# Spreading the loads of x and of the mixing weights over the expert slots, and a loading depth of three groups in the last stage of a two-layer mixture kernel

## What is computed

```python
x = x + L0_ffn(L0_cond(x, cond_128, ...), W_gate, b_gate, W_e, b_e)      # mean of relu(x @ W_e + b_e) over the top 2
x = x + L1_ffn(L1_cond(x, cond_128, ...), qweight, scales, zeros, bias)  # (mix_b @ x_b) @ (scales * q - zeros) + bias
```

## Time and profile before

| | us |
|---|---|
| median of 3 timed runs | 529.42 (529.12 to 530.06) |
| the profiled execution's own time | 527.31 |
| its span, first to last instruction | 525.5 |
| TensorE busy | 499.7 (95% of the span) |
| VectorE busy | 347.2 (66%) |
| ScalarE busy | 121.3 (23%) |
| GpSimd busy | 152.8 (29%) |

### The profile page before, as it was taken

One profiled execution on the slowest core, in us unless ns is written; L12 is line 12 of the kernel. 1 busy time (PEld: TensorE's weight loads), 2 busy tenths in 40 slices (PEclk: granted clock), 3 DMA queues, 4 the chain that ended last, 5 costly groups with the idle time before them and its releaser, 6 DMA issues. The chain is left out here.

```text
span 525.5 us, 10384 instructions
## 1 busy us (share of the span) xinstructions
PE 499.7 (95%) x2412; PEld 332.3 (63%) x2413; DVE 347.2 (66%) x1082; ACT 121.3 (23%) x277; POOL 152.8 (29%) x178
## 2 busy tenths in 40 slices
PE   6999999999999987999999999999997599999996
PEld 5999999999954433444444444444445477777774
DVE  3688888888865637574443545443346499999996
ACT  3233333334411101111111111111123112222220
POOL 9144444444446222232333232332223000000000
PEclk9999999999998998999999999999998989999999
DMA  4979978999766795556666656565435988988522
GB/s 118 286 206 306 299 255 274 345 362 319 211 179 204 221 269 140 137 145 176 181 174 172 166 162 178 173 188 146 141 111 202 334 312 277 291 286 276 204 83 100
DMA packets 91440, 113.06 MB, mean 215 GB/s; under 512 B 25438, under 2 KB 62222, under 8 KB 90372
## 3 DMA queue, kind: packets, MB, share of 16 engines
q1 hardware_dynamic: 73200, 71.26, 47.9%
q0 software_dynamic: 11664, 36.24, 18.9%
q10 hardware_dynamic: 6536, 5.10, 3.6%
HBM read 67.55 MB, written 46.52 MB: 217 GB/s over the span
## 5 line engine op out<-in xcount | busy, mean ns | idle before, releaser
L1190 PE MATMUL bank<-we,lT 128*128 x536 | 235.4, 600 | 4.5 <-DVE ring_a L929 4.5
L1190 PEld LDWEIGHTS bank<-we,lT 128*128 128x128 f32 x536 | 102.4, 192 | 132.8 <-issue 132.6
L540 POOL DMA_INDIRECT pairs_d<-ring_b,pair_i x71 | 70.7, 995 | 166.2 <-DVE pair_i L918 97.9
L929 DVE TENSOR_TENSOR ring_a<-bank,be_bc 128x512 f32<-128x512 f32 x71 | 49.0, 691 | 104.0 <-PE bank L1190 59.2
L1163 PE MATMUL bank<-wconv,phases 128*128 128x128 f32 x768 | 91.4, 276 | 0.7 <-ACT phases L566 0.7
L619 ACT ACTIVATE ring_b<-ring_a 128x512 f32<-128x512 f32 x71 | 44.8, 631 | 201.2 <-DVE ring_a L929 185.8
L1163 PEld LDWEIGHTS bank<-wconv,phases 128*128 128x128 f32 x768 | 88.7, 192 | 0.9 <-ACT phases L566 0.9
L523 POOL DMA_INDIRECT lists_d<-token_list,row_i x64 | 62.9, 982 | 83.3 <-DVE row_i L839 48.4
L915 DVE STREAM_TRANSPOSE lT<-xt 128x512 f32<-128x512 f32 x71 | 49.9, 703 | 10.5 <-DMA keys<-lists_d 8.9
L1257 PE MATMUL bank<-wq,high 128*128 128x512 f32 x128 | 38.9, 427 | 3.4 <-PEq L1205 3.4
L1151 PE MATMUL bank<-wg,lT 128*128 128x136 f32 x256 | 37.4, 289 | 1.1 <-DVE partial L810 1.1
(11 more groups left out here) (194 smaller groups left out, 401.7 us busy)
## 6 DMA issues: line engine op xcount, KB each, us to landing
xt<-lists_d SPq DMA_DIRECT2D x284, 64.0 KB
xt<-in_x SPq DMA_DIRECT2D x60, 256.0 KB
we<-pairs_d SPq DMA_DIRECT2D x28, 512.0 KB, 5.0
we<-in_L_ffn_W_e SPq DMA_DIRECT2D x8, 1024.0 KB
out<-orow_list SPq DMA_DIRECT2D x32, 256.0 KB, 3.7
lists_d<-orow_list SPq DMA_DIRECT2D x8, 257.0 KB
be_bc<-in_L_ffn_b_e ACTq DMA_DIRECT2D x4, 512.0 KB
words<-pairs_d POOLq DMA_DIRECT2D x4, 512.0 KB, 5.4
```

The source lines that it names most:

```text
L540: pool.indirect_dma_start(pairs_d, bass.IndirectOffsetOnAxis(ap=pair_i[:, s % DR:s % DR + 1], axis=0), ring_b[:, s % U, :], None, bounds_c ...
L929: dve.tensor_tensor(ring_a[:, j % 2, :], ps_exp[j % 2][:, :], be_bc[:, bass.ds(expert, 1), :].rearrange("p a n -> p (a n)"), ALU.add).then ...
L1190: mm = pe.matmul(ps_exp[j % 2][:, :], lT[:, j, p * P:(p + 1) * P], we[:, bass.ds(expert, 1), p, :].rearrange("m a n -> m (a n)"), start=(p ...
```

## The change

Four edits.

- SyncE, stage 2: the loads of x of groups 0 to 3 no longer stand together after `list_step(7)`; one stands after each of `list_step(16)` to `list_step(19)`. The unrolled part of SyncE's loop is longer by 12 slots for this.
- ScalarE, stage 2: the two loads of the mixed biases move from slot 8 to slot 9; the four loads into `mix_bd` move from slot 8 to slots 11, 15, 19 and 23, one in each. ScalarE's unrolled part is longer by 16 slots.
- SyncE, start of stage 3: x of group 4, then pairs 4, x 5, pairs 5, x 6, pairs 6, in place of four loads of x and eight of pairs. The waits for the scatters stay with pairs 4, 5 and 6.
- SyncE, `row_step(g)`: after the store of group g it loads x and pairs of group g + 7 (DEPTH = 3), in place of x of g + 8 and pairs of g + 12.

No transfer is added or taken away; the sizes and the buffers are the same. The programs of VectorE, TensorE and GpSimd are unchanged.

```diff
--- before.py
+++ after.py
@@ -31,6 +31,7 @@
 U = 4
 XR = 4
 FR = 8
+DEPTH = 3
 DR = 8
 LK = L + 2
 NO_PAIR = 1 << 20
@@ -435,11 +436,12 @@
                                      ).then_inc(list_in[ja], 16)
                     sp.dma_start(keys[:, ja, :], lists_d[bass.ds(row, P), L:LK]).then_inc(list_in[ja], 16)
 
-            for s in range(-U, lo2):
+            for s in range(-U, 20):
                 list_step(s, s % U)
-            for g in range(PRIMED):
-                sp.dma_start(htok[:, g, :], x_g[g]).then_inc(x3_in[g % XR], 16)
-            stepped(sp, list_step, lo2, lo2, hi2 - U, NT - U)
+                if s >= 16:
+                    g = s - 16
+                    sp.dma_start(htok[:, g, :], x_g[g]).then_inc(x3_in[g % XR], 16)
+            stepped(sp, list_step, 20, 20, hi2 - U, NT - U)
 
             def load_x(a):
                 sp.dma_start(xt[:, a % XR, :], x_g[a]).then_inc(x3_in[a % XR], 16)
@@ -448,25 +450,24 @@
                 sp.dma_start(found[:, a % FR, :, :], pairs_g[a]).then_inc(pairs_in[a % FR], 16)
 
             sp.wait_ge(lT_ready, NT)
-            for g in range(PRIMED, PRIMED + XR):
-                load_x(g)
+            load_x(PRIMED)
             sp.wait_ge(exp_done, NT)
-            for g in range(PRIMED, PRIMED + FR):
-                if filled_by(g - 1) < NT:
-                    for i, done in enumerate(result_out):
-                        sp.wait_ge(done, 16 * len(range(i, min(filled_by(g), NT), U)))
+            for g in range(PRIMED, PRIMED + DEPTH):
+                for i, done in enumerate(result_out):
+                    sp.wait_ge(done, 16 * len(range(i, min(filled_by(g), NT), U)))
                 load_pairs(g)
+                if g + 1 < PRIMED + DEPTH:
+                    load_x(g + 1)
 
             def row_step(g, j):
                 sp.wait_ge(out_ready, g + 1)
                 sp.dma_start(out_g[g], orow[:, j % 2, :]).then_inc(out_out[j % 2], 16)
-                a, b = g + PRIMED + XR, g + PRIMED + FR
-                if live(a, NG):
-                    sp.wait_ge(ya_ready, a - XR + 1)
+                a = g + PRIMED + DEPTH
+                if a < NG:
+                    wait(sp, ya_ready, a - XR + 1)
                     load_x(a)
-                if live(b, NG):
-                    sp.wait_ge(y_ready, b - FR + 1)
-                    load_pairs(b)
+                    wait(sp, y_ready, a - FR + 1)
+                    load_pairs(a)
 
             unrolled(row_step, 0, NG)
             for s in out_out:
@@ -626,19 +627,21 @@
                 act.dma_start(mixb_d[1], mixb_lo[:, :].bitcast(F32)).then_inc(mix_out, 16)
                 act.dma_start(mix_d, mix_sb[:, :, :]).then_inc(mix_out, 16)
 
-            def load_mix():
-
-                act.wait_ge(mixbd_zero, 1)
+            def load_mix_bias():
+
                 act.wait_ge(mix_out, 48)
                 act.wait_ge(mixb_one, 1)
                 for half in range(2):
                     pair = 2 * B + 2 * half
                     act.dma_start(token_rows[pair:pair + 2, :].bitcast(F32),
                                   mixb_d[half:half + 1].rearrange("a n c -> a (n c)").to_broadcast((2, N * C))).then_inc(mix_in, 16)
-                for s in range(SUB):
-                    rows = slice(s * C, (s + 1) * C)
-                    act.dma_start(mix_bd[rows, :, rows],
-                                  mix_d.rearrange("(g s) i o -> s i g o", s=SUB)[s]).then_inc(mix_in, 16)
+
+            def load_mix(s):
+
+                act.wait_ge(mixbd_zero, 1)
+                rows = slice(s * C, (s + 1) * C)
+                act.dma_start(mix_bd[rows, :, rows],
+                              mix_d.rearrange("(g s) i o -> s i g o", s=SUB)[s]).then_inc(mix_in, 16)
 
             for s in range(lo2):
                 step2(s, s % U)
@@ -651,10 +654,13 @@
                     act.dma_start(bias_bc[:, :], bias.rearrange("(a n) -> a n", a=1).to_broadcast((P, L))).then_inc(q_in, 16)
                 if s == 6:
                     store_mix()
-            for s in range(lo2, 12):
+            for s in range(lo2, 28):
                 step2(s, s % U)
-                if s == 8:
-                    load_mix()
+                if s == 9:
+                    load_mix_bias()
+                if s in (11, 15, 19, 23):
+                    load_mix((s - 11) // 4)
+
             def step3(g, j):
                 if live(g, NG):
 
@@ -668,7 +674,7 @@
                     wait(act, lin_done, a - 1)
                     act.copy(high[:, ja, :], ps_mix[ja][:, :]).then_inc(high_ready, 1)
 
-            stepped(act, step2, 12, 12, hi2, hi2)
+            stepped(act, step2, 28, 28, hi2, hi2)
             for s in range(hi2, NT):
                 step2(s, s % U)
                 if s == 60:
```

## The result

| | before | after |
|---|---|---|
| median of 4 runs, us | 529.27 (527.73 to 530.06) | **515.31** (514.04 to 515.49) |
| span of the profiled execution, us | 525.5 | 513.4 |
| TensorE busy, us | 499.7 | 496.1 |
| mean granted clock | 0.982 | 0.995 |

The ratio of the times is 0.9734, with a 95% interval of 0.9707 to 0.9762: 12.6 to 15.5 us less, where 13.1 were forecast. The medians lie 14.0 us apart, the two profiled spans 12.1. What follows accounts for those 12.1 us. The landing of a transfer is its completion, and a landing time is counted from the issue.

A forecast was written before the change was run, and what follows sets the result against it. TensorE, busy 95% of the span, was taken as the bound, its waits as what counts; VectorE paces stage 3 from group 2. -7.5 + 0.2 - 4.5 - 1.3 = -13.1 us from 529.42 gives 516.3 us, range 514.6 to 519.6.

The forecast's parts named there:

- The store waited for its turn behind six loads: Start of stage 3, SyncE's queue: group 0's store took 8.73 us behind pairs 6 to 11; fewer loads ahead give -7.5 us.
- The residual wait: VectorE before L1027 of group 2: +0.2 us charged for group 0's store, between nothing and 1.0 us.
- x and pairs three groups ahead are enough: Stage 3: loads have 10.0 us before use, pairs took 4.5 to 6.3 us, so the smaller depth costs nothing.
- List 12: Stage 2, slot 12: without x loads ahead it lands by 193.3; -4.5 us with slot 11, -2.7 if list 11 comes no sooner.
- the -1.3 us of the clock: Stage 2 behind slot 12: without gaps TensorE's clock stays up, four slots taking 13.8 us instead of 15.03; bounds 0 and -1.3.
- List 11 at 187.5: Stage 2, slot 11: the list lands at 187.5 instead of 189.1, so TensorE's 1.78 us wait goes.
- the bound without gain: Stage 2, list 11: landing bounded by 189.1, no gain, and 186.7, a gain of 2.4 us.
- The 1.75 us of ScalarE for each block load: Stage 2: each block load takes 1.75 us of ScalarE's issuing between relus of 0.63 us, and fits.
- The 3.4 us gap between stages 2 and 3 ... do not move: Sum of the prediction: the start, this gap and the end stay as they are.
- The third rival: Stage 3: three groups too few; at 12 us landing a step takes 4.33 us, +16 us, near 532.5; chance 0.02.

The follow-up runs named there:

- The two runs on list 11: Changed kernel with the blended kernels' store moved from slot 6 to 10, 513.64 us; besides that, packed weights loaded in slots 0 to 3, 513.59 us.
- the run of all edits together: Changed kernel plus store of group 0 before the last-scatter wait, blended kernels' store in slot 10, packed weights in slots 0 to 3: 513.50 us.
- the run with early weights: Changed kernel with the blended kernels' store in slot 10 and packed weights, scales, zeros and biases loaded in slots 0 to 3: 513.59 us.
- stage 2 alone: Kernel before with only the loads of x and of the mixing weights spread, last stage loading as before: 522.48 us, ratio 0.9889.

## Why the prediction was right, and where it was not

- *The store waited for its turn behind six loads.* Right in its main step, which is shown in two ways: with one load ahead the store lands after 4.66 us, and in another queue it passes loads. "Its turn" is not all of it: in the other queue, with the six loads in flight, a store still took 6.80 us. Of the 7.5 us of waiting, 5.6 + 0.6 = 6.2 went (the marks for groups 2 and 5). The residual wait was taken at 0.2 us, with a bound of 1.0, and measured at 1.31. Two things were off. The store landed 0.6 us behind pairs 6, as worked out, but pairs 6 took 4.4 us in place of 3.6, so that the store landed 5.0 us behind their issue and not 4.3. And the output of group 0 began 3.6 us before pairs 6 were issued, where it had been 2.6 us, so the buffer was wanted 1.0 us sooner against them.
- *x and pairs three groups ahead are enough.* Right. With two nothing is waited for either. The Trainium skill's rule of early issue ("DMA: Bandwidth & Descriptors", section on rules for kernel authors) says nothing of how early; that it asks for the depth of 8 was the prediction's reading, and the traces speak against that reading. One group ahead cost 15.9 us, as a load issued too late should, but beyond two groups the deeper loads bought nothing and cost 6.9 us of a store's wait.
- *List 12.* The -2.7 us for slot 12 and the -1.3 us of the clock came: no wait, clock 1.00 at 200 to 204. The mark of the last bias add gives 4.7 us for stage 2 where 5.8 were summed; what is missing is list 11.
- *List 11 at 187.5.* This step failed. It read "what moves ... shared the engines with it for most of that time". List 11 landed at 189.2, and 1.59 of the 1.78 us stayed, as at the bound without gain. The two runs on list 11 show what shared the engines: what stayed in place, packed weights and bias broadcast above all, and the blended kernels' store. With all of it moved and no late start, in the run of all edits together, the wait was gone.
- *The 1.75 us of ScalarE for each block load* was mis-sized: one alone is issued in 0.31 to 0.34 us. It cost nothing either way.
- *"The 3.4 us gap between stages 2 and 3 ... do not move".* The gap did not, but the clock behind it did, which no edit explains (last section): luck, but worth little. The output of group 0 came 1.5 us sooner by it, and then waited at the store. From the last bias add to the output of group 2 the changed kernel took 17.62 us (407.90 - 390.28), and the run with early weights, whose clock fell and which waited for no store, 17.81 (408.16 - 390.35). From that bias add to the output of group 5 the marks give 1.5 + 5.6 + 0.6 = 7.7 us, where the sum had 7.5 - 0.2 = 7.3.
- *The third rival* had the point of decision near enough (a distance of 10 us; by the recurrence of the run with one group ahead the wait begins at 4 x 3.68 - 4.4 = 10.3) and its price too high: 12 us of landing would give (4.4 + 12) / 4 = 4.1 us a step, not 4.33.
- The two profiled executions are 12.1 us apart, the sum said 13.1. The medians are 14.0 apart. That 515.31 comes so near to the 516.3 forecast is in part luck: the profiled execution missed its own forecast of 514.2 by 1.0 us, and the 2.1 us that the forecast added between profile and median were 0.1 in the changed kernel (515.17 and 515.31). Both are inside what the runs of the kernel before scatter.

## What to carry to other kernels

Where loads and stores share one queue, count the bytes that are issued ahead of the first store that a small ring of output buffers waits for; prefetch to the distance that covers one landing (here two groups) and not to the size of the ring. A wait in the issuing engine's program, such as that for a last scatter, belongs behind the stores that are ready before it. And where an input arrives late, look at everything in flight with it, and first at what was issued before it: moving the neighbours that came after it did nothing for list 11.

## What the hardware showed beside that

**The same gap, with and without a fall of the clock.** All 14 traces (13 programs, the changed kernel twice) have a TensorE gap of 3.3 to 3.4 us between stages 2 and 3. In the kernel before the clock fell behind it, in the changed one it did not; stretches with the granted clock as the third number from the right, before and then after:

```profile
397.00:399.00 2.00, 1.22 (x3) 1.05 (x4) 1.72 (x5) 1.31 (x3) 1.66 (x2) 0.69 0.51 57
399.00:401.00 2.00, 2.00 (x6) 1.52 (x6) 0.48 (x1) 0.17 (x1) 1.35 (x3) 0.50 0.89 349
```

```profile
393.00:395.00 2.00, 1.45 (x7) 1.24 (x7) 1.72 (x4) 1.23 (x2) 1.47 (x2) 1.00 0.47 32
395.00:397.00 2.00, 2.00 (x14) 1.83 (x13) 0.88 (x2) 0.10 (x1) 1.54 (x2) 1.00 1.01 407
```

Behind the gap the granted clock fell to 0.50 (1.2 GHz) in 9 of the 14 traces and stayed at 1.00 (2.4 GHz) in 5, among them both of the changed kernel and the one with stage 2 alone. Where it fell the first output came 10.4 us or more behind the last bias add of the table, where not 8.8 to 8.9. These 1.5 us are not an effect that the change can be credited with: versions that differ from it only in the last stage show both. What decides it is open.

A second place shows the same. Three early slots (24 matmul rows, from 158.6 to 161.9 us on) took 12.3 us in 9 of the 14 traces, the kernel before and both of the changed one among them, and 10.6 us in 5; in two of these 5 it was slot 0 that took 5.4 us in place of 3.7. In the trace after the granted clock was 0.50 from 160 to 162 us, in the one with all edits together 1.00. The run with the x loads back in one piece and the one with one group ahead are among the 5, so these 1.7 us, too, cannot be credited to moving the weights.

**Issuing takes longer in a burst and beside other loads.** Block loads of equal shape were issued in 0.31 to 0.34 us each when spread (trace after), 0.93 (3.71 / 4) in a burst, and 1.75 (7.02 / 4) in a burst beside 1 MB of x. The share of the transfer engines alone does not tell which: it was 0.94 over that burst, 1.06 over the one beside x, and 0.96 where the last of the spread ones was issued in 0.31 us. In the trace after, the 1 KB keys load of list 11 took 1.60 us to issue at a share of 1.02, where 0.35 is usual.

**GpSimd's stores** landed about as fast as SyncE's (median 3.9 us of all 32, against 3.7 us of 27 later stores of SyncE), but the span ended 7.5 us after the last of them.
